# Where a feed-forward layer's weights are split into two parts: in the stage before it, or in its first units

## The reference, cut to what matters

```python
x = x + gat(ctx, layernorm(x), ...)             # 1: graph attention
x = x + experts(layernorm(x), ...)              # 2: 8 experts, 2 of them per token
x = x + context_attention(layernorm(x), ctx, ...)   # 3
xn = layernorm(x)                               # 4: feed-forward, 512 -> 2048 -> 512
h = silu(xn @ w_gate) * (xn @ w_up)
h = keep_the_2_largest_of_4(h)                  # by magnitude, in groups of 4 neighbours
x = x + h @ w_down
```

## Time and profile before

| what | value |
|---|---|
| median of 3 runs | 1055.85 us (1054.09 to 1061.31) |
| the profiled execution | 1056.58 us, span 1054.8 us |
| graph attention, routing | 0 to 158 us |
| experts' stage | about 158 to 448 us |
| First | about 448 to 486 us |
| units | about 486 to 1055 us |
| TensorE busy | 953.1 us, 90% of the span |
| VectorE, ScalarE, GpSimd busy | 649.3, 388.2 and 358.1 us |

### The profile page before, as it was taken

How to read it: one execution, slowest core, us unless ns; L and a number is a source line. 1 busy time by engine, 2 the same in 40 slices (tenths; PEclk the granted TensorE clock), 3 DMA queues, 4 the chain that set the end, 5 groups by cost and what they waited for, 6 DMA issues and landing times.

```text
span 1054.8 us, 14952 instructions
## 1 busy us (share of the span) xinstructions
PE 953.1 (90%) x4628; PEld 796.5 (76%) x4628; DVE 649.3 (62%) x1441; ACT 388.2 (37%) x682; POOL 358.1 (34%) x439
## 2 busy tenths in 40 slices
PE   4996719999998989947999999999999999999997
PEld 3873418888988878835778888888888888888885
DVE  7986754342242544484695895776858957665446
ACT  4876234443453543332343332432333324222121
POOL 0466024575566665542141221321211211101120
PEclk8998859999999999976999999999999999999999
DMA  8478119887788864355457334475172642545551
GB/s 340 157 148 225 56 46 366 292 300 279 253 312 308 291 231 145 109 183 166 160 163 236 101 100 160 164 231 164 40 240 104 216 160 80 166 154 163 195 160 41
DMA packets 68801, 195.26 MB, mean 185 GB/s; under 512 B 8161, under 2 KB 8289, under 8 KB 67489
## 3 DMA queue, kind: packets, MB, share of 16 engines
q0 software_dynamic: 41392, 129.78, 38.8%
q1 hardware_dynamic: 27312, 64.34, 17.2%
HBM read 146.12 MB, written 50.60 MB: 186 GB/s over the span
## 4 chain that ended last, share of the span: by engine, by line
PE 68%; DVE 7%; DMA 3%; issue 3%; POOL 2%; ACT 2%; DVEq 0%; ACTq 0%; POOLq 0%
PE ps L78 22%; PE ps L79 21%; PE ps L80 21%; DMA w_scratch<-pre 3%; POOL dn_w_lo L1576 1%; PE ps L1626 1%; PE ps L1958 1%; PE ps L1651 1%; DVE gu_w_lo L1801 1%; DVE raw L2558 1%; POOL pre L1582 1%; DVE raw L2574 1%; PE ps L2154 0%; DVE logits L2244 0%; DVE dn_w_hi L1832 0%
## 5 line engine op out<-in xcount | busy, mean ns | idle before, releaser
L78 PE MATMUL ps<-f_x_lo,f_w 128*128 128x512 f32 x512 | 200.9, 392 | 3.2 <-DVE raw L1443 1.8
L79 PE MATMUL ps<-f_x_hi,f_w 128*128 128x512 f32 x512 | 200.2, 391 | 0.0
L80 PE MATMUL ps<-f_x_hi,f_w 128*128 128x512 f32 x512 | 200.1, 391 | 0.0
L1437 ACT ACTIVATE moe_rows<-ps 128x512 f32<-128x512 f32 x64 | 38.1, 596 | 227.7 <-PE ps L80 227.7
L1443 DVE TENSOR_TENSOR raw<-moe_rows,ps 128x512 f32<-128x512 f32 x64 | 43.9, 686 | 126.1 <-PE ps L80 118.5
L78 PEld LDWEIGHTS ps<-f_x_lo,f_w 128*128 128x128 f32 x512 | 96.7, 189 | 24.0 <-issue 2.1
L78 PE MATMUL ps<-gu_w_lo,m_xT_hi 128*128 (+1 forms) x312 | 105.3, 338 | 9.3 <-issue 6.4
L80 PEld LDWEIGHTS ps<-f_x_hi,f_w 128*128 128x128 f32 x512 | 96.7, 189 | 20.2
L79 PEld LDWEIGHTS ps<-f_x_hi,f_w 128*128 128x128 f32 x512 | 96.7, 189 | 19.9
L78 PE MATMUL ps<-f_w,kv_c_hi 128*128 128x512 f32 x256 | 102.4, 400 | 2.3 <-DVE x L2593 2.3
L79 PE MATMUL ps<-f_w,kv_c_lo 128*128 128x512 f32 x256 | 101.7, 397 | 0.0
(11 more groups left out here) (350 smaller groups left out, 1975.6 us busy)
## 6 DMA issues: line engine op xcount, KB each, us to landing
f_w<-w_scratch POOLq DMA_DIRECT2D x52, 1024.0 KB, 5.7
f_w<-w_scratch POOLq DMA_DIRECT2D x52, 512.0 KB, 5.5
w_scratch<-pre POOLq DMA_DIRECT2D x32, 768.0 KB, 5.0
pre_raw<-in_ffn SPq DMA_DIRECT2D x32, 384.0 KB, 6.4
raw<-in_moe_gu SPq DMA_DIRECT2D x32, 352.0 KB, 4.3
y_scratch<-m_y SPq DMA_DIRECT2D x39, 256.0 KB, 3.4
raw<-in_moe_dn SPq DMA_DIRECT2D x24, 256.0 KB, 4.5
x<-in_x SPq DMA_DIRECT2D x4, 1024.0 KB, 10.9
```

Of the source, the lines that this page charges most:

```text
L78: eng.matmul(out, lhs_hi, rhs_lo, start=start, stop=False)
L79: eng.matmul(out, lhs_lo, rhs_hi, start=False, stop=False)
L80: return eng.matmul(out, lhs_hi, rhs_hi, start=False, stop=stop)
L1437: act.activation(sg[:, k % 2, :], self.gate_bank(n, r), ACT.Silu).then_inc(self.silu, 1)
```

## The change

The chunks of the experts' stage are cut from 32 to 8: quarter 0 only (`CHUNKS = 2 * RQ`). Chunk m is loaded in block 3m + 3 and split in block 3m + 6, so blocks 6, 9, ... 27 have one. The other three quarters (`FRESH`) are split inside the units, straight into the buffers `w[r]`, where they are used. The work comes in 18 pieces: 12 of gate and up (128 x 1024) and 6 of down (two tiles of 128 x 512). Each piece is loaded by SyncE (512 KB) into one of three staging buffers, rounded by ScalarE into `w_hi`, subtracted by GpSimd into `w_lo`, and stored by SyncE (1 MB) into `w_scratch` for the later sequences. The fetches of splits 1 to 3 (12 of 1 MB, 12 of 512 KB) go. Pieces 0 to 3 stand in unit 0, 4 to 7 in unit 1, 8 to 13 in unit 2 (down and gate/up in slots 1 and 2, gate/up alone in slots 3 and 4), 14 and 15 in unit 3, 16 and 17 in unit 4.

```diff
-CHUNKS, CW = 2 * Q * RQ, 3 * D // 2
+CHUNKS, CW = 2 * RQ, 3 * D // 2
+FRESH = tuple(range(1, Q))
...
+        self.stage = [outer["raw"][:, 4 * D:6 * D]] + [outer["fresh_raw"][:, k, :] for k in range(2)]
...
+    def pieces(n, slot):
+
+        down = (("down", n - 1, slot - 1),) if n - 1 in FRESH and slot <= RQ // 2 else ()
+        gate_up = (("gate_up", n + 1, slot - 1),) if n + 1 in FRESH else ()
+        return down + gate_up
...
+    def load_piece(self, sp, piece):
+        kind, s, i = piece
+        at, t = self.place[piece], RQ * QUARTER[s]
+        if at >= 3:
+            sp.wait_ge(self.raw_lo, at - 2)
+        if kind == "gate_up":
+            sp.dma_start(self.stage[at % 3], self.raw[t + i][:, 0:2 * D]).then_inc(self.raw_got[at % 3], 16)
...
+    def keep_piece(self, sp, piece):
+        kind, s, i = piece
+        t = RQ * QUARTER[s]
+        sp.wait_ge(self.raw_lo, self.place[piece] + 1)
+        if kind == "gate_up":
+            sp.dma_start(self.store[t + i, :, :, 0:2, :], self.w[i][:, :, 0:2, :].bitcast(F32)).then_inc(self.kept_gu[i], 16)
...
+    def act_piece(self, act, piece):
+        kind, s, i = piece
+        at, stage = self.place[piece], self.piece_stage(piece)
+        act.wait_ge(self.raw_got[at % 3], 16 * (at // 3) + 16)
+        if kind == "gate_up":
+            act.wait_ge(self.products, RQ * (FIRST[s] - 1) + i + 1)
+            if s >= 2:
+                act.wait_ge(self.kept_gu[i], 16 * (s - 1))
+            act.copy(self.w_hi[i][:, 0:2, :], stage).then_inc(self.raw_hi, 1)
+        else:
+            act.wait_ge(self.acc_done, TB * FIRST[s])
...
+    def pool_piece(self, pool, piece):
+        kind, s, i = piece
+        stage = self.piece_stage(piece)
+        pool.wait_ge(self.raw_hi, self.place[piece] + 1)
+        if kind == "gate_up":
+            pool.tensor_tensor(self.w_lo[i][:, 0:2, :], stage, self.w_hi[i][:, 0:2, :].bitcast(F32), ALU.subtract
+                               ).then_inc(self.raw_lo, 1)
...
+    def wait_gate_up(self, pe, n, r):
+        s = SPLIT[n]
+        if s in FRESH:
+            pe.wait_ge(self.raw_lo, self.place["gate_up", s, r] + 1)
...
@@ -1507,12 +1604,14 @@
+        LOADS, SPLITS = ({3 * m + at: m for m in range(CHUNKS)} for at in (3, 6))
...
-                if g <= CHUNKS:
-                    chunk_hi(j, i)
+                if g in SPLITS:
+                    chunk_hi(SPLITS[g])
...
@@ -2387,6 +2483,14 @@
+            order = list(u.place)
+            sp.wait_ge(first.sim_done, TB)
+            for piece in order[:2]:
+                u.load_piece(sp, piece)
+            for k, piece in enumerate(order):
+                if k + 2 < len(order):
+                    u.load_piece(sp, order[k + 2])
+                u.keep_piece(sp, piece)
...
@@ -2411,22 +2515,28 @@
             first.pool(pool)
             for r in range(1, RQ):
-                u.fetch_gate_up(pool, 1, r - 1)
                 slot_work(r)
-            u.fetch_gate_up(pool, 1, RQ - 1)
+                split_pieces(0, r)
+            split_pieces(0, RQ)
...
                 for r in range(RQ):
                     for s in new(n + 1):
-                        u.fetch_gate_up(pool, s, r)
+                        if s not in FRESH:
+                            u.fetch_gate_up(pool, s, r)
                     if r < RQ - 1:
                         slot_work(6 * n + r + 1)
+                    split_pieces(n, r + 1)
...
@@ -2508,9 +2626,12 @@
                     late(6 * n + r)
+                    if r >= 1:
+                        split_pieces(n, r)
                 early(6 * n + 4)
                 size(n, 0)
                 size(n, 1)
+                split_pieces(n, RQ)
                 early(6 * n + 5)
```

More of the change, by code:

```diff
@@ L1367, in __init__ @@
         self.acc_done, self.acc_free = sem(tag + "acc_done"), sem(tag + "acc_free")
+        self.raw = outer["dram"]["ffn"]
+        self.stage = [outer["raw"][:, 4 * D:6 * D]] + [outer["fresh_raw"][:, k, :] for k in range(2)]
+        self.raw_got = [sem(f"{tag}raw_got{k}") for k in range(3)]
+        self.raw_hi, self.raw_lo = sem(tag + "raw_hi"), sem(tag + "raw_lo")
+        self.kept_gu, self.kept_dn = ([sem(f"{tag}kept_{name}{r}") for r in range(RQ)] for name in ("gu", "dn"))
+        self.place = {}
@@ new lines, in __init__, with piece_stage @@
+        for n in range(UNITS):
+            for slot in range(1, RQ + 1):
+                for piece in self.pieces(n, slot):
+                    self.place[piece] = len(self.place)
+    @staticmethod
+    def pieces(n, slot):
+        down = (("down", n - 1, slot - 1),) if n - 1 in FRESH and slot <= RQ // 2 else ()
+        gate_up = (("gate_up", n + 1, slot - 1),) if n + 1 in FRESH else ()
+        return down + gate_up
+    def piece_stage(self, piece):
+        return self.stage[self.place[piece] % 3].rearrange("p (k n) -> p k n", k=2)
@@ new lines, in pool_piece @@
+    def pool_piece(self, pool, piece):
+        kind, s, i = piece
+        stage = self.piece_stage(piece)
[3 more added lines that the diff above has]
+                               ).then_inc(self.raw_lo, 1)
+        else:
+            for k, r in enumerate((2 * i, 2 * i + 1)):
+                ins = pool.tensor_tensor(self.w_lo[r][:, 2, :], stage[:, k, :], self.w_hi[r][:, 2, :].bitcast(F32),
+                                         ALU.subtract)
+            ins.then_inc(self.raw_lo, 1)
@@ new lines, in loads, with wait_down @@
+    @staticmethod
+    def loads(s):
+        return s + 1 - sum(f <= s for f in FRESH)
+    def wait_gate_up(self, pe, n, r):
+        s = SPLIT[n]
+        if s in FRESH:
+            pe.wait_ge(self.raw_lo, self.place["gate_up", s, r] + 1)
+        else:
+            pe.wait_ge(self.got_gu[r], 16 * self.loads(s))
+    def wait_down(self, pe, n, r):
+        s = SPLIT[n]
+        if s in FRESH:
+            pe.wait_ge(self.raw_lo, self.place["down", s, r // 2] + 1)
+        elif self.down_at(n) == 2:
+            pe.wait_ge(self.got_dn[r], 16 * self.loads(s))
+        else:
+            pe.wait_ge(self.got_last[r], 16)
@@ L1508, in pipeline, with chunk, chunk_pair @@
                 body(g, (g - 1) % 4, (g - 1) // 4)
[L1510 to L1515, removed]
+        def chunk(m):
+            return dram["ffn"][m // 2][:, CW * (m % 2):CW * (m % 2) + CW]
+        def chunk_pair(m):
+            return outer["w_store"][m // 2][:, :, CW * (m % 2):CW * (m % 2) + CW]
+        LOADS, SPLITS = ({3 * m + at: m for m in range(CHUNKS)} for at in (3, 6))
         def kvT(b):
@@ L2412, in slot_work, with split_pieces @@
                     later.fetch(pool, h, 1)
+            def split_pieces(n, slot):
+                for piece in u.pieces(n, slot):
+                    u.pool_piece(pool, piece)
             first.pool(pool)
             for r in range(1, RQ):
-                u.fetch_gate_up(pool, 1, r - 1)
                 slot_work(r)
-            u.fetch_gate_up(pool, 1, RQ - 1)
+                split_pieces(0, r)
+            split_pieces(0, RQ)
             for n in range(1, UNITS):
                 for s in new(n - 1):
-                    if s >= 1:
+                    if s >= 1 and s not in FRESH:
                         for r in range(RQ):
@@ L2492, in round_hid, with split_pieces @@
                     act.copy(hid_hi[:, r, :], hid[:, r, :]).then_inc(u.hid_hi_done, 1)
+            def split_pieces(n, slot):
+                for piece in u.pieces(n, slot):
+                    u.act_piece(act, piece)
             first.act(act)
```

77 lines of the change are left out of this document (46 added, 31 removed).

## The result

The change makes the kernel slower by about 1%: 1065.42 us (median of 7 runs, 1064.78 to 1070.37) against 1054.26 for the kernel before in the runs beside it, a ratio of 1.0114 (95% interval 1.0091 to 1.0136). I had predicted 1058, with a range of 1042 to 1069. Against the kernel before, that was a change of +2 us; the measured one is +11. The profiled execution of the kernel after took 1070.37 us (span 1068.6), the longest of its seven. A second profile of it (`e5_change_again`, span 1065.4) shows the same waits.

The account below looks back on a forecast made before the run. In the units TensorE, always busy from 600 to 700 us, was taken as the bound, so only its new waits count. 1056.6 - 18 + 2.4 + 6.7 + 8 + 3.4 = 1059.1 profiled, 1058 against the median; range 1042 to 1069.

Parts of the forecast that it names:

- The gain, 18 us: Experts' stage: with 24 of 32 chunks gone, casts no longer wait for stores; 18 us gained, bounds 15 to 20.
- Hold of VectorE: Units 0 and 1: GpSimd's subtractions stall VectorE's two-operand instructions, up to a full 2.39 us a piece; lower bound nothing.
- Unit 0 to 1: Piece 3's subtraction falls in the middle of `keep_two(0, 1)`, delaying `hidden(1, 0)` and TensorE; costs 2.4 us in full.
- Unit 1 to 2: Pieces 4 to 7 make VectorE about 9.2 us late at `hidden(2, 0)`; costs 6.7 us after slack, lower bound 0.
- Unit 2, the load: Piece 11's load waits for a staging buffer and a store, holding ScalarE's cast of turned rows; 8 us, 4 to 9.9.
- Units 3 and 4 cost nothing: Two pieces each in units 3 and 4 have 3 to 5 us of slack before TensorE; nothing charged.
- The clock: After the units' three new waits, the clock drops to half speed; two drops charged, 3.4 us, bounds 0 and 7.
- Case A: The forecast, chance 0.51: both new waits come, costs of 15 to 25 us about eat the gain; 1048 to 1065.
- Case C: Slower rival, 0.14: VectorE doesn't recover in unit 2, TensorE stands again in unit 3; 8 to 12 us more, 1066 to 1071.
- B: Faster rival, 0.26: `keep_two` is not held, unit 2's wait comes whole or in part; 1041 to 1047.
- E: Rival, 0.05: neither a hold of VectorE nor a wait of note in the units; 1038 to 1040.
- D: Rival, 0.04: the experts' stage's excess belongs to expert weights' loads, not chunks; gain 5, costs 20, 1070.

Follow-up runs that it names:

- e5_change_again: The kernel after, unchanged, run and profiled once more on another chip than the first four experiments: 1066.49 us, ratio 1.0123 to the kernel before.
- e1: Kernel after with quarters 1 to 3 not split at all, the units fetching quarter 0's split tiles instead: 1042.66 us, ratio 0.984 to before.
- e4: Kernel before, all 32 chunks in the experts' stage, with a third buffer for split chunks: 1057.36 us, ratio 0.9965 to before.
- e2: Kernel after with GpSimd subtracting 8 columns of each piece in place of 1024: 1055.54 us, ratio 0.9958 to before.
- e8: Kernel after with GpSimd filling the low parts with zeros, writing without reading, in place of subtracting: 1053.81 us, one run.
- e3: Kernel after with both down pieces of units 3 and 4 split in the unit's first slot: 1063.09 us, ratio 1.0037 to before.
- e6: Kernel after with VectorE subtracting the pieces and both down pieces of units 3 and 4 in slot 1: 1049.36 us, ratio 0.9971 to before.
- e7: Kernel after with only quarters 2 and 3 split in the units, 16 chunks in the stage, down pieces in slot 1: 1050.52 us, ratio 0.998 to before.
- e9: As e7, but VectorE subtracts the pieces in place of GpSimd: 1045.47 us, ratio 0.9916 to before.
- e10: As e9, but only quarter 3 is split in the units and 24 chunks stay in the stage: 1046.99 us, ratio 0.9923 to before.

## Why the prediction was right, point by point

**The gain, 18 us: right in size.** 16.5 us by the profiles, 17 by e1. Its reasoning was right in part. The six us of blocks 28 and 29 went with GpSimd's subtraction off `kv_c_lo`. 2.8 of them are the wait for `kv_c_lo`; the rest is read from the blocks' length, and no run took the subtraction alone away there. For the 13.3 us of the blocks before I made the casts' waits for stores the carrier; e4 gives them 4, and 2.9 us are still there in after (183.56 us for the 27 blocks against 180.7).

**Hold of VectorE: right in the mechanism, by the trace, e2 and e8; in unit 1 to 2 twice too large.** The upper bound that I took is the measured one. Unit 0 to 1: 2.4 predicted, 2.2 measured (3.96 less 1.76). Unit 1 to 2: 6.7 predicted, 3.3 measured. The holds themselves came as forecast, on the first `keep_two` of unit 1: pieces 5 and 6 are subtracted by 537.1, and its compares end at 538.9 in place of 535.3; piece 7 holds the masked products of 540.80, which take 3.64 us in place of 1.43. That makes 5.8 us where I had 6.0. What did not come are the 3.1 us by which this `keep_two` was to start late. TensorE wanted the hidden part of unit 2 at 550.92 here (554.21 less its wait of 3.29) and at 562.17 before, 11.25 us later. Moved by these 11.25 us, the compares of 533.42 start at 544.67, and before's started at 544.85: not late at all. The 3.1 us were added up without the 2.8 us that TensorE itself loses at half clock behind the first wait (its distance to before shrinks from 14.04 to 11.25 us between the two waits). I charged the clock to the sum, but gave VectorE no slack for it. The Trainium skill's rule (SBUF — State Buffer, "Who interferes with whom"), that a GpSimd instruction which reads SBUF contends with VectorE's instructions of two SBUF inputs and one that only writes does not, agrees with e2, e8 and the pair under e8. The other half of what the prediction quotes, that the later one blocks, agrees in part. In the rows of after it is VectorE's instruction that starts later and is held (523.45 after 522.69, 533.42 after 532.39). In the earlier trace rows it starts first, at 377.52 against 378.03, and is held all the same, while GpSimd's takes its usual 1.82 us; there the measurement goes against the page.

**Unit 2, the load: right.** 8 us predicted, 7.4 measured, by the mechanism named: ScalarE stands at piece 11 for 7.13 us, with the cast of the turned rows behind it. From the end of piece 8's subtraction (565.36) to that cast (572.34) it is 7.0 us, the figure that I took for store and load together. How much of it is the late buffer and how much the load's own time behind the store, no run separates; in e2, where buffers come free 2.3 us a piece sooner, 5.0 us stay.

**Units 3 and 4 cost nothing: wrong.** This is the step that failed: "their places in the queues have 3 to 5 us of slack before TensorE". It cost 7.8 us. The slack was read for pieces that GpSimd could start at once; the second down piece has the norm and two fetches of its slot ahead of it, and these come late by themselves: in the kernel before the norm's step on GpSimd starts at 608.96 and the fetches end at 612.83, while the down product starts at 609.73. An estimate from these rows alone would have been 612.83 + 2.5 for the piece - 609.73 = 5.6 us. e3 takes the wait away by moving the piece one slot forward.

**The clock: mis-sized.** 3.4 us predicted. The units lost 30.3 us and the new waits make 2.2 + 3.3 + 7.4 + 7.8 = 20.7; the remaining 9.6 have no wait. Behind each of the four the clock is at half (after, columns as above; the one behind 554.21 is not shown):

```profile
513.00:517.00 4.00, 2.80 (x7) 2.25 (x8) 3.97 (x7) 2.60 (x5) 0.00 (x0) 0.50 0.01 2
...
575.00:579.00 4.00, 3.75 (x15) 3.56 (x16) 0.79 (x2) 1.84 (x3) 2.59 (x2) 0.50 1.05 414
621.00:625.00 4.00, 3.29 (x8) 2.64 (x9) 0.00 (x0) 0.00 (x0) 0.32 (x1) 0.50 0.64 250
```

I charged two drops for three waits, and there were four. In windows of 1 us the clock is back at full 5.6, 3.1, 6.0 and 3.9 us after TensorE's restart. That is 18.6 us of work at half clock, of which half, 9.3, is lost: the 9.6. So a drop cost 1.6 to 3.0 us and not 1.7. The experiments agree: units longer than before's by 12.9 us with 8.7 of new waits (e2), 14.1 with 9.9 (e8), 20.8 with 14.1 (e3), 12.1 with 9.0 (e6), 10.0 with 7.2 (e7). Taken together the new waits of a kernel cost 1.3 to 1.5 times their length. Not each one does: in e6 the clock is 1.00 in all windows from 500 to 560, though TensorE waits 3.2 us there, up to 508.21.

**The sum.** 1059 was predicted from -18 + 2.4 + 6.7 + 8 + 3.4 = +2.5 us. Measured, profile against profile: -16.5 + 2.2 + 3.3 + 7.4 + 7.8 + 9.6 = +13.8. The three terms of the units that I named came to 17.1 against 12.9; the sum was short by the wait in unit 3 and by the clock, and the profiled execution is itself 5 us above its median. Case A, the forecast, had three of the four waits with their mechanisms, but its costs, 15 to 25 us, were 30.3, and 1065.42 lies at the very end of its own 1048 to 1065. That the time is inside the recorded range owes something to the width of that range, 27 us, and to the 3.4 us too much in unit 1 to 2, which hid a part of what was missing. By the 1% that I took as measurable, 1.0114 lies on the border between "same", to which I gave 0.56, and "slower", to which I gave 0.19. Case C had the right place, unit 3, and a wrong cause: VectorE did recover, and GpSimd's queue was what TensorE waited for. B and E needed `keep_two` not to be held, and it was. D laid the stage's excess on the expert weights, and e1 has the gain with these unchanged.

## What to carry to other kernels

Before work is moved into another engine's queue, look up for every instruction moved what stands ahead of it in that queue and when that is ready, not only when the engine is idle; the wait that I foresaw (piece 11 ahead of a cast) and the one that I did not (piece 15 behind a norm) are both of that kind. A subtraction on GpSimd is not free for VectorE: here the same work on VectorE itself took half as long and made the kernel 7 us faster (e6 against e3, e9 against e7). And of work that crowds a stage, take out as much as makes it fit, and no more: with VectorE subtracting, the kernel was 0.8% faster than before with one or two of the four quarters moved (e10, e9), and 0.3% with three (e6).

## What was not expected of the hardware

**Waits of TensorE cost the clock as well:** 0.3 to 0.5 us for each us waited, summed over the new waits of each of six kernels, which are 0.5 to 8 us long. It is not a fixed price of each wait: the 3.3 us in unit 2 of after were followed by a clock of 0.50, the 3.2 us in unit 1 of e6 by one of 1.00. In e9, whose new waits are 1.1 and 1.6 us, the clock is 1.00 in the windows from 510 to 580.

**ScalarE stood for 4 to 5 us with no cause in the trace** (3.9 in e4) in the profiles of e1 to e4 and at one place, the gate's activation in the block that makes the third of the four keys; in the profiles of before, after, e5 to e10 it did not. In e3:

```profile
411.59 0.46 ACT L1804 ACTIVATE m_sg<-ps 128x352 f32<-128x352 f32 x1 [5.24 <-DMA xn_scratch<-g_xn]
...
414.80 1.11 PE L1725 MATMUL ps<-ident,moe_rows 128*128 128x128 f32 x4 [4.13 <-DVE kv_c_raw L1906]
```

The releaser named there ended long before; in e2 the same gap is 4.59 us and has no releaser but issue. The four kernels differ in both stages and ran on one chip, on which the kernel before had a median of 1061.21 us and times of 1051.36 to 1064.9; on the other two it had 1052.44 and 1054.46. It is no matter of e3's edit, which e6 and e7 contain as well, and it goes with the chip as far as the ten profiles of the experiments tell; the chip of the first two profiles is not on record, and what it is stays open.
